# A decoder layer on one core: cross scores from f16 high and low halves, weight splits and hidden splits shared with ACT and POOL

## The reference

```python
def _L0_xattn_ref(x, context, Wq, Wk, Wv):
    q = x @ Wq.T; k_raw = context @ Wk.T; v_raw = context @ Wv.T
    ...
    q = _rmsnorm(q); k = _rmsnorm(k)          # per head of 16
    scores = jnp.einsum('bhnd,bhmd->bhnm', q, k) * HEAD_DIM ** (-0.5)
    attn = jax.nn.softmax(scores, axis=-1)
    out = jnp.einsum('bhnm,bhmd->bhnd', attn, v)
x = x + _L0_attn_ref(_layernorm(x), ...)      # 16 heads of 128, 4 kv heads, rope, causal
x = x + _L0_xattn_ref(_layernorm(x), ctx, Wq, Wk, Wv)
x = x + _L0_ffn_ref(_layernorm(x), W_up, W_gate, W_down)   # silu(up) * gate, ternary weights
```

## Time and profile before

| | us |
|---|---|
| median of 3 runs (1392.16 to 1394.27) | 1393.27 |
| the profiled execution | 1391.79 |
| its span | 1389.7 |

### The profile page before, as it was taken

One profiled execution on the slowest core, in us unless ns is written; L12 is line 12 of the kernel. 1 busy time (PEld: TensorE's weight loads), 2 busy tenths in 40 slices (PEclk: granted clock), 3 DMA queues, 4 the chain that ended last, 5 costly groups with the idle time before them and its releaser, 6 DMA issues.

```text
span 1389.7 us, 27539 instructions
## 1 busy us (share of the span) xinstructions
PE 1314.8 (95%) x10968; PEld 867.6 (62%) x10968; DVE 784.6 (56%) x1942; ACT 640.9 (46%) x1452; POOL 274.8 (20%) x266
## 2 busy tenths in 40 slices
PE   7689999999999999999999999999999779999996
PEld 6456666666666666566666666666666446565543
DVE  6987776777677775434445434444346784444422
ACT  3243354333333355366666666666667223232321
POOL 0244452434244441111111111111111000000000
PEclk9799999999999999999999999999999999999999
DMA  8400000000000003111111111112203410000000
GB/s 267 161 1 1 1 1 1 1 1 1 1 1 1 1 1 124 47 58 63 46 46 46 46 45 46 45 47 68 66 25 139 159 68 23 0 24 1 23 1 28
DMA packets 23604, 59.99 MB, mean 43 GB/s; under 512 B 1214, under 2 KB 10811, under 8 KB 20405
## 3 DMA queue, kind: packets, MB, share of 16 engines
q1 hardware_dynamic: 23477, 58.24, 12.6%
HBM read 54.96 MB, written 3.28 MB: 42 GB/s over the span
## 4 chain that ended last, share of the span: by engine, by line
PE 84%; DVE 6%; issue 3%; ACT 1%; DVEq 0%; ACTq 0%
PE A L1616 21%; PE A L1529 11%; PE C L1940 10%; PE A L1583 10%; PE C L1640 6%; PE B L1657 5%; PE C L1569 3%; PE C L1554 3%; PE A L1956 2%; PE B L1956 2%; PE A L1538 2%; PE B L1625 2%; PE B L1562 2%; PE B L1546 2%; DVE qk L1120 1%
## 5 line engine op out<-in xcount | busy, mean ns | idle before, releaser
L1616 PE MATMUL A<-wxhl,arena 128*122 128x512 f16 x1152 | 265.3, 380 | 0.0
L1616 PEld LDWEIGHTS A<-wxhl,arena 128*122 128x122 f16 x1152 | 149.1, 134 | 88.0 <-issue 8.3
L1940 PE MATMUL C<-arena 128*128 128x375 f16 (+1 forms) x1024 | 188.2, 337 | 5.1 <-DVE arena L1121 5.1
L1529 PE MATMUL A<-arena,wxhl 128*125 128x512 f16 (+1 forms) x780 | 174.9, 382 | 6.1 <-DVE tub L960 4.3
L1940 PEld LDWEIGHTS C<-arena 128*128 128x128 bf16 x1024 | 100.4, 98 | 82.7 <-issue 9.6
L506 POOL TENSOR_TENSOR arena<-arena,region 100x512 f32<-100x512 f32 (+1 forms) x64 | 65.9, 1062 | 421.2 <-DVE region L1084 421.2
L690 ACT ACTIVATE arena<-C 122x1600 f32<-122x1600 f32 x96 | 144.3, 1503 | 4.4 <-PE C L1640 2.8
L1529 PEld LDWEIGHTS A<-arena,wxhl 128*125 128x125 f16 (+1 forms) x780 | 105.0, 137 | 65.7 <-DVE tub L960 4.8
L482 POOL TENSOR_TENSOR region<-tub 125x512 f32<-125x512 f32 (+1 forms) x65 | 82.6, 1270 | 265.4 <-DVE tub L960 265.3
L618 ACT ACTIVATE region<-C,negm 100x100 f32<-100x100 f32 x256 | 84.3, 358 | 102.2 <-DVE negm L1004 102.2
L1583 PE MATMUL A<-arena,stageb 128*125 128x512 f16 (+1 forms) x416 | 123.8, 379 | 0.7 <-ACT arena L674 0.7
(11 more groups left out here) (163 smaller groups left out, 2096.5 us busy)
## 6 DMA issues: line engine op xcount, KB each, us to landing
stageb<-in_wffn SPq DMA_DIRECT2D x16, 768.0 KB, 4.7
arena<-in_ctxt SPq DMA_DIRECT2D x16, 722.0 KB, 4.7
stageb<-in_wffn SPq DMA_DIRECT2D x6, 1024.0 KB, 4.8
wxhl<-in_wffn SPq DMA_DIRECT2D x6, 1024.0 KB, 4.8
arena<-in_wqkv SPq DMA_DIRECT2D x4, 1024.0 KB, 15.4
arena<-in_wx SPq DMA_DIRECT2D x3, 1024.0 KB, 6.9
out_x<-xres SPq DMA_DIRECT2D x12, 250.0 KB
xres<-in_x SPq DMA_DIRECT2D x1, 2250.0 KB
```

Source lines behind the costliest of these rows:

```text
L1529: ins = pe.matmul(A[j % 2][0:m, :], xp[:, k, at:at + m], wp[:, j, k, :], start=(n == 0), stop=(n == 11))
L1616: ins = pe.matmul(A[(par + n) % 2][0:rows, :], lhs, wp[:, 0 if n == 0 else 1 if n < 4 else 2, k, :], start=(i == 0), stop=(i == 11))
L1940: ins = pe.matmul(C[2 * (e % 2) + half][:, 0:cols], wf[:, 3 * (e // 4) + half, k, (e % 4) * 128:(e % 4 + 1) * 128], part[:, k, 0:cols], st ...
```

## The change

1. Start. Blocks 5, 6, 8 and 7 of the weights are scaled by ACT (`w_scaled`) and their low part is made by POOL (`w_lo` there); DVE keeps block 9 and the three cross blocks. Two of the five multiplications by the reciprocal root of tile 0 go from POOL to ACT (`z_part`). The rope tables are made earlier on DVE. PE gets 14 matmuls on zeros at the start and 14 on the identity after `values_of(0)`, whose results nothing reads.
2. Queries are projected by tiles of 125 rows (`project_q`, 13 of them) instead of by batches of 100 (16).
3. Keys and queries are split after the norm: `kx` holds for each head 16 high and 16 low f16 values side by side (`key_hi` on ACT, `key_lo` on DVE); `qx` holds the high values twice and the low values twice (`query_hi`, `query_lo`). Transposes are f16, in eight groups of four heads; queries are turned by tile (`turn_queries`, twice eight), keys by batch (`turn_heads`, four times six). All copies out of B[0] are DVE's. Each head has a 32-row tile of its own, and a unit of scores is 32 f16 matmuls of 100 columns.
4. In a turn, `scores2(b + 1, 0)` comes after `attend2(b, 3)` instead of before it.
5. Feed forward, first unit: `hidden_lo` is POOL's.

The diff, cut to its core:

```diff
-        kT = carve([128, NT, CTXP])
+        kT = carve([128, 2 * NT, CTXP], F16)
...
+            n = unit_cols(0)
+            for e in range(ET):
+                pool.wait_ge(*count("a_hh", 0, e + 1))
+                if e >= 2:
+                    pool.wait_ge(*count("pe_dn", 0, e - 1))
+                pool.tensor_tensor(hl[e % 2][:, 0:n], hd[e % 2][:, 0:n], hh[e % 2][:, 0:n], ALU.subtract)\
+                    .then_inc(g_hl, 1)
...
+            for j in (0, 2, 4):
+                z_of(0, j, 2 if j else 1)
+            w_lo(6, 2)
+            w_lo(8, 3)
+            w_lo(7, 4)
...
+            def query_hi(i, par):
+                n = rows_of(i)
+                act.wait_ge(*count("g_qn", i, 1))
+                act.wait_ge(*count("pe_qT", i - 1, 2))
+                q = raw[par][0:n, 3].rearrange("p (h d) -> p h d", h=XH).unsqueeze(2).broadcast_to([n, XH, 2, XD])
+                act.activation(qx[0:n, 0].rearrange("p (h f d) -> p h f d", h=XH, f=2), q, ACT.Copy)\
+                   .then_inc(sig["a_qh"], 1)
+            def key_hi(b, c, par):
+                act.wait_ge(*count("g_kn", b, c + 1))
+                act.wait_ge(*count("pe_T", b - 1, 4))
+                act.activation(kx[c][:, :, 0, :], raw[par][0:KC, c].rearrange("p (h d) -> p h d", h=XH), ACT.Copy)\
+                   .then_inc(sig["a_kh"], 1)
...
                 if end < 2:
+                    if q_tile(b + 1) is not None:
+                        query_hi(q_tile(b + 1), odd)
                     values(b + 1, 0, odd)
+                    key_hi(b + 1, 0, odd)
                     magnitudes(b, 0, par)
...
+            def key_lo(b, c, par):
+                dve.wait_ge(*count("a_kh", b, c + 1))
+                dve.tensor_tensor(kx[c][:, :, 1, :], raw[par][0:KC, c].rearrange("p (h d) -> p h d", h=XH),
+                                  kx[c][:, :, 0, :], ALU.subtract).then_inc(sig["d_kl"], 1)
+            def keys_back(b, t):
                 dve.wait_ge(*count("pe_T", b, t + 1))
                 dve.wait_ge(*count("pe_sc", b - 1, T_UNITS[t]))
+                dve.tensor_copy(kT[:, 2 * t:2 * t + 2].rearrange("p g n -> p (g n)"), B0h[:, 0:2 * CTXP])\
+                   .then_inc(sig["d_T"], 1)
...
                 for e in range(ET):
-                    hidden_lo(u, e)
+                    if not first:
+                        hidden_lo(u, e)
...
-                for f in range(2):
-                    t, c = divmod(2 * u + f, NC)
-                    for r in range(RT):
-                        ins = pe.matmul(C[r][0:KC, f * 2 * S:(f + 1) * 2 * S],
-                                        kT[32 * r:32 * r + 32, t, c * KC:(c + 1) * KC],
-                                        qm[32 * r:32 * r + 32, t].rearrange("p f s -> p (f s)"), start=True, stop=True)
+                for f in range(4):
+                    g, c = divmod(4 * u + f, NC)
+                    for half in range(2):
+                        for r in range(RT):
+                            ins = pe.matmul(C[r][0:KC, f * S:(f + 1) * S], kT[32 * r:32 * r + 32, g, c * KC:(c + 1) * KC],
+                                            qTs[b % 2][32 * r:32 * r + 32, g, half, :], start=(half == 0), stop=(half == 1))
```

More of the change, by code:

```diff
@@ L224, in build @@
         carve = carver()
-        raw = [carve([KC, 4, 512]) for _ in range(2)]
+        raw = [carve([TW, 4, 512]) for _ in range(2)]
         ctxs = carve([128, KT, CTXP])
@@ L277, in build @@
         osum = carve([TW, DM])
+        kx = [carve([KC, XH, 2, XD], F16) for _ in range(2)]
         carve = carver(region2)
@@ L585, in w_hi, with w_scaled, z_part @@
                 act.activation(dst, src, ACT.Copy, scale=SW).then_inc(a_whi, 1)
+            def w_scaled(j):
+                act.activation(staged(j)[0], staged(j)[0], ACT.Copy, scale=SW).then_inc(a_ws, 1)
+            def z_part(j):
+                act.wait_ge(*count("d_rstd", 0, 1))
+                act.wait_ge(*count("g_w", 0, j + 1))
+                for h in range(4):
+                    z = zb[:, j, h * D:(h + 1) * D]
+                    ins = act.activation(z, z, ACT.Copy, scale=rstd[:, 4 * j + h:4 * j + h + 1])
+                ins.then_inc(a_z, 1)
             def x_hi(i, bank):
@@ L780, in _ @@
                 values(0, c, 0)
+            query_hi(0, 0)
+            for c in range(NC):
+                key_hi(0, c, 0)
             ctx_hi(1)
-            keys_back(0, 0)
-            keys_back(0, 1)
             x2_hi(1, B[0])
@@ L804, in turn @@
                 out_back(b, 0)
-                keys_back(b, 3)
                 if end < 2:
@@ L838, in turn @@
                     ctx_hi(b + 2)
+                out_back(b, 2)
+                out_back(b, 3)
                 if end < 2:
                     exp2(b + 1, 0)
-                out_back(b, 3)
-                if end < 2:
-                    keys_back(b + 1, 1)
-                if end < 1:
-                    keep_raw(b + 2, 0, par)
+                if x2_tile(b) is not None:
+                    keep_q(x2_tile(b), par)
                 if end < 1:
@@ L1341, in _ @@
             row_stats2(1)
-            for n in range(2):
-                square_sums(0, n)
+            square_sums_q(0)
+            square_sums(0, 1)
             for g in range(4):
@@ L1351, in _ @@
             normed2(1, rs1[:, 0:1])
-            ctx_lo(1)
+            query_lo(0, 0)
+            for c in range(NC):
+                key_lo(0, c, 0)
             queries_back(0, 0)
             queries_back(0, 1)
+            ctx_lo(1)
+            keys_back(0, 0)
+            keys_back(0, 1)
             add_attn(TL - 1, A[0])
             x2_lo(1, B[0])
-            square_sums(1, 0)
+            square_sums_q(1)
             def turn(b, par, end):
                 odd = 1 - par
+                if end == 2:
+                    dve.wait_ge(*count("a_abs", NB - 1, 3))
+                    dve.tensor_reduce(fsc[:, 0:3], asum[:, :, :, 0], AX.X, ALU.add).then_inc(d_fsc, 1)
+                keys_back(b, 2)
                 if end < 2:
                     square_sums(b + 1, 1)
-                else:
-                    dve.wait_ge(*count("a_abs", NB - 1, 3))
-                    dve.tensor_reduce(fsc[:, 0:3], asum[:, :, :, 0], AX.X, ALU.add).then_inc(d_fsc, 1)
-                queries_back(b, 2)
                 if x2_tile(b) is not None:
@@ L1374, in turn @@
                     x3_lo(0, 0, A[0])
-                queries_back(b, 3)
+                keys_back(b, 3)
                 if end < 2:
@@ L1403, in turn @@
                     ternary(2, 0)
+                if end < 2 and q_tile(b + 1) is not None:
+                    queries_back(q_tile(b + 1), 0)
+                    queries_back(q_tile(b + 1), 1)
                 if end < 2:
-                    queries_back(b + 1, 0)
+                    keys_back(b + 1, 0)
                 if end == 1:
@@ L1413, in turn @@
                 if end < 2:
-                    queries_back(b + 1, 1)
-                if end < 1:
-                    square_sums(b + 2, 0)
+                    keys_back(b + 1, 1)
+                if x2_tile(b) is not None:
+                    square_sums_q(x2_tile(b))
                 if o2_tile(b) is not None:
@@ L1593, in x2_turn, with project_q @@
                 ins.then_inc(sig["pe_xT2"], 1)
+            def project_q(i, par):
+                m, at, n = rows_of(i), i % 4 * TW, 0
+                pe.wait_ge(*count("d_x2", i, 1))
+                for xp, wp in ((x2h, wxh), (x2h, wxl), (x2l, wxh)):
+                    for k in range(KT):
+                        ins = pe.matmul(A[par][0:m, :], xp[:, k, at:at + m], wp[:, 0, k, :], start=(n == 0), stop=(n == 11))
+                        n += 1
+                ins.then_inc(sig["pe_q"], 1)
@@ L1677, in x3_turn @@
                 ins.then_inc(sig["pe_xT3"], 1)
+            pe.wait_ge(d_warm, 1)
+            for _ in range(WARM):
+                pe.matmul(B[0][:, 0:128], vv[:, 0:128], vv[:, 0:128], start=True, stop=True)
             pe.wait_ge(ld_c, 16)
@@ L1692, in _ @@
                 project(0, j)
-            pe.wait_ge(d_wlo, 1)
+            pe.wait_ge(g_wlo, 1)
             pe.wait_ge(*count("d_u", 0, 4))
             values_of(0)
+            for _ in range(FILL):
+                pe.matmul(B[1][:, 0:128], ident, ident, start=True, stop=True)
             def heads_back(b, j):
```

348 lines of the change are left out of this document (215 added, 133 removed).

## The result

| | before, us | after, us |
|---|---|---|
| median of 4 runs each, same chip | 1393.77 | 1418.76 (1417.95 to 1420.72) |
| the profiled execution | 1391.79 | 1420.72 |
| its span | 1389.7 | 1418.7 |

The account below looks back on a forecast made before the run. PE was taken to bound cross attention, DVE the start and first feed-forward unit. Start -7, feed forward -7 and cross attention +10 (-30 + 34 + 6) gave -4 us: 1388 profiled, 1389 median, range 1364 to 1411.

Parts of the forecast that it names:

- The size of a unit of scores: Cross attention: 32 f16 matmuls, bound by weight loads at 54 ns a round, take 0.57 us instead of 0.88.
- rival 2: Cross attention scores bound by issue, about 25 ns a matmul, 0.95 us a unit: +24 us, 1413, slower kernel; chance 0.27.
- PE's work, -30: Cross attention over 16 batches: fewer projections, faster scores and key transposes, less added query transposes and tile changes: -30 us.
- Late exponentials, +34: Cross attention: ACT's unit 4 exponentials wait behind query_hi and others, so PE stands ahead of unit 5: +34 us.
- Two smaller waits, +6: Cross attention: uncovered `keys_back` in four turns, 4 us, and moved `queries_back` and `out_back` in twelve, 2 us.
- The start, -7: Start: first self-attention exponentials come earlier, after ACT's copy of block 9 ends at 66.4 instead of 73.0: -7 us.
- Feed forward, -7: First feed-forward unit: DVE loses high and low part work over twelve steps, less POOL's interference: -7 us, ends -12 and 0.
- The sign that the prediction named: First feed-forward unit: two steps in 8 to 9 us, with the first ternary instruction longer than 0.75.
- Rival 1: Cross attention: the exponentials are not late, 1355, or half of it, 1372; chance 0.18 with its half.
- 3: Start and feed forward: POOL takes back what it is given, start -3, feed forward 0, time 1400; chance 0.13.
- 4: Start: idle matmuls leave the clock as it is, moving the forecast 1 us at most; no separate chance given.

Follow-up runs that it names:

- filled_hole: Changed kernel plus idle matmuls on PE (nine or three a turn) in the hole ahead of unit 5 of the scores; 1402.62 us, ratio 1.0073 to the kernel before.
- old_late: Kernel before, with ACT making the first values copy eight times instead of once, so unit 4's exponentials end late; 1471.79 us, ratio 1.0481 to the kernel before.
- old_start: Kernel before with part 1 of the change (the start) alone; 1388.88 us, ratio 0.9961 to the kernel before.
- old_ffn_pool: Kernel before with part 5 of the change alone (`hidden_lo` of the first feed-forward unit on POOL); 1386.53 us, ratio 0.9946 to the kernel before.
- no_warm: Changed kernel without its idle matmuls at the start (both sets of 14 removed); 1411.95 us, ratio 1.0138 to the kernel before.
- reordered_no_warm: reordered without the 14 idle matmuls ahead of the first centring; 1371.20 us, ratio 0.9836 to the kernel before.
- all_behind: Changed kernel with unit 4's exponentials first on ACT, ahead of query_hi, values, key_hi and magnitudes, and add_cross before key_lo on DVE; 1387.14 us, ratio 0.9958 to before.
- reordered: all_behind with the lists of PE, ACT and DVE reordered, projection 6 split around the query transposes; 1372.59 us, ratio 0.9845 to the kernel before.
- mag_behind: Changed kernel with ACT's `magnitudes` moved behind the exponentials of unit 4 in each cross turn; 1419.82 us, ratio 1.0197 to the kernel before.
- some_behind: Changed kernel with query_hi alone left ahead of unit 4's exponentials on ACT, and add_cross before key_lo on DVE; 1393.97 us, ratio 1.0009 to the kernel before.

## Why the prediction was wrong, by its own steps

**The size of a unit of scores: right.** 0.58 against 0.57 us. By the start times a round of four follows the last after 56 ns, where 54 was forecast (the prediction's own working gives some 50, and doesn't say how it became 54), and the four of a round start 3 to 4 ns apart. The rival of 25 ns a matmul would give 0.8 for 32; the trace has 18 ns each in the mean. The rule of the Trainium skill (TensorE: Matmul & The Clock Gate, "Wait — 56ns, not 53.3ns?") doesn't hold for these matmuls on four row tiles, and rival 2 falls. The prediction held that the weighted sums' mean of 24 ns did not decide; the single starts in that trace would have, as the four of a round start 7 ns apart there and the rounds 86.

**PE's work, -30: right.** 464.6 - 434.7 = 29.9 us in 15 turns.

**Late exponentials, +34: the stand right, its price wrong.** In turns with queries unit 5 starts at T0 + 10.98 to 11.07 (11.59 in the last), where 9.27 - 0.62 + 2.3 = 10.95 was forecast, and the stands sum to 33.8 us. The terms fit one by one: 2.3, 2.7, 2.9, 3.5 and 0.8 were forecast, and PE is idle for 2.24, 2.77, 2.68, 3.29 and 0.75 to 0.83 in these turns, to which each return to work adds 0.2. So it wasn't luck. The failed step is the sentence "Now PE stands 2.3 us in a turn" as the whole cost of it: the forecast's sum has no term for the clock. Behind such stands the granted clock was at the lower level for 47.8 us of these turns, which cost 22.0. The earlier trace rows had 1.00 there because PE had no hole; that number was a product of the order that the change broke, not a property of the stage. filled_hole and old_late show cause and effect from both sides; that the loss is half of the low time is the account's own rule, and filled_hole, which has the stand without the low clock, bears it out: its 15 turns are 22.0 - 3.7 = 18.3 us shorter, its median 16. The 22 us are more than the whole distance from the range's end (1411) to the result (1418.8). Without them the kernel would be at some 1397, an estimate: in the range, but no faster than before.

**Two smaller waits, +6: too small.** The bare `keys_back` cost 3.1 (forecast 4). The move of `out_back` and `queries_back` was put at 0.2 us in twelve turns; it was 0.5 in fifteen ahead of the fourth weighted sum, as the key transposes that cover `out_back` now take 0.35 us and it also stands behind `values` on ACT. With 2.2 ahead of the query transposes, for which the forecast had no term, and 1.2 in small ones the waits other than the stand are 14.2, +12.2 over the 2.0 of the kernel before. That brings the stage to -29.9 + 33.8 + 12.2 + 22.0 = 38.1, and 39.3 with its ends.

**The start, -7: too large.** 3.9 in the profile and 4.6 by old_start, inside its ends of 3 and 10. ACT's copy of block 9 (L624) was to end at 66.4; it ends at 68.1, against 73.1 before, and the first exponentials follow it:

```profile
66.22 1.91 ACT L624 ACTIVATE arena<-alo 128x2048 f16<-128x2048 f32 x1 [3.13 <-POOL arena L530]
68.04 0.33 ACT L669 ACTIVATE region<-C,negm 100x100 f32<-100x100 f32 x1
```

```profile
37.61 4.42 DVE L1308 TENSOR_TENSOR wxhl<-region 125x384 f32<-125x384 f32 x1
...
47.30 0.55 DVE L1308 TENSOR_TENSOR wxhl<-region 125x384 f32<-125x384 f32 x1
...
64.46 5.73 DVE L1090 TENSOR_SCALAR negm<-smax 100x4 f32<-100x4 f32 x2
```

```profile
37.23 4.37 POOL L530 TENSOR_TENSOR arena<-arena 128x2048 f16<-128x2048 f32 x1
...
66.09 4.07 POOL L530 TENSOR_TENSOR arena<-stageb,arena 128x2048 f16<-128x2048 f32 x1
```

The mis-sized term is POOL's time. Its first split (37.23 to 41.6) holds DVE's table product for 4.42 us that takes 0.55 alone (47.30), ahead of the norm of tile 0; POOL is done with its three multiplications at 58.0 and not 55.5, and its two splits take the lower end of the forecast's 4.1 to 5.1 each. DVE's own chain was off by more, but wasn't the last: its row maxima begin at 62.5 and not at 56.6 (the prediction names three splits of 2.3 and takes off two). Behind the exponentials' start POOL's last split then holds DVE's negated maxima: 5.73 us for two instructions of four columns, 1.70 and 4.12, to the moment when POOL is done (66.09 + 4.07).

**Feed forward, -7: right.** -6.4, and -7.2 in old_ffn_pool. Two steps take 8.78 us against 9.86; POOL's subtraction (0.91) holds a ternary instruction of 1.29 to 1.92, as put. The sign that the prediction named, the first ternary instruction above 0.75, did not show; it is the second, L1242, that is held:

```profile
1129.15 1.29 DVE L1242 SCALAR_TENSOR_TENSOR arena<-wxhl,fsc,qk 128x1024 bf16<-128x1024 f32 x1
...
1131.65 1.92 DVE L1242 SCALAR_TENSOR_TENSOR arena<-stageb,fsc,qk 128x1024 bf16<-128x1024 f32 x1
```

**The rivals.** None was the case. Rival 1 (exponentials in time) fell with the hole; 3 did not happen (start and feed forward gave 10.3 us together); of 4, the idle matmuls, no gain is shown: the first exponentials start at 68.0 us with them and at 68.3 in no_warm. Whether they move the clock is open: 6.8 us are low until then against 13.7 in no_warm, but in reordered_no_warm, without the first 14, it is 3.4. The result has the sign of rival 2, but another mechanism.

## What to carry to other kernels

Where TensorE is without holes and another engine's instruction becomes late, price the hole twice: its length, and the matmuls behind it at the lower clock; here the second was two thirds of the first, and a quarter in old_late, with larger holes. Ask it of every added wait that recurs, and put what PE waits for ahead of what nobody waits for on the engine that makes it: that and a split projection of PE's turned +1.8% into -1.5% with the same instructions (all_behind and reordered). After a wait is shortened, look for the next releaser in the same place before you count the gain.

## What was not expected of the hardware

- Holes of 2.2 to 3.3 us in twelve of 15 turns of some 34 us, in a PE that is otherwise mostly busy, took the granted clock to its lower level for 47.8 us; in mag_behind holes of 1.6 to 2.2 did as much. The Trainium skill (TensorE: Matmul & The Clock Gate, "HAM oscillation — how this bites in real kernels") gives as its abstract rule idle gaps longer than these; here shorter ones did it, and the measurement decides. In the profiled executions of some_behind, filled_hole and reordered, with smaller holes, the clock stayed whole in these turns; in that of all_behind 6.8 us were low.
- With nearly the same waits (48.0, 48.3, 48.5 and 50.4 us in the changed kernel, mag_behind, no_warm and old_late) the low clock was 47.8, 47.8, 34.1 and 27.3 us. What decides it was not settled.
- Two `TENSOR_SCALAR` on four columns took 5.73 us beside POOL's splits: on DVE the length of the own work is no guard. It is in line with the Trainium skill (SBUF — State Buffer, "SBUF: two separate sides"), by which the loser of the shared ports blocks wholly.
- 32 matmuls of 100 columns on four row tiles go in 0.58 us, 18 ns each in the mean: four start 3 to 4 ns apart, and the rounds 56.
